# One elementwise product of 128x768 made in eight operations of 128x96, in the third layer of a graph network kernel

## What is computed

```python
def _L2_gnn_ref(feat, src, dst, W, b):
    m = jax.nn.relu(feat[src]) + EPS
    logits = BETA * m
    seg_max = jax.ops.segment_max(logits, dst, num_segments=N)
    ex = jnp.exp(logits - seg_max[dst])
    denom = jax.ops.segment_sum(ex, dst, num_segments=N)
    a = ex / denom[dst]
    msg = jax.ops.segment_sum(a * m, dst, num_segments=N)
    feats = feat + msg
    return feats @ W + b
x = _layernorm(x + _L2_gnn_ref(x, L2_gnn_W, L2_gnn_b, src, dst), axis=-1)
```

## Time and profile before

| | |
|---|---|
| median of 3 runs | 4265.86 us |
| lowest and highest | 4262.5 and 4268.29 us |
| span of the profiled execution | 4261.0 us |
| DVE busy, whole span | 2819.2 us (66%) |
| POOL busy, whole span | 2740.4 us (64%) |
| third layer, first gather to the end of the stage | 2443 to 3110 us |

### The profile page before, as it was taken

The page is one execution under the profiler, slowest core; times in us unless marked ns, Lnnn a source line. Parts: engine busy times, 40 slices in busy tenths (PEclk is TensorE's granted clock), DMA queues, the critical chain, the costliest instruction groups (busy, mean ns, idle before and its releaser), DMA issues. The chain is left out here.

```text
span 4261.0 us, 39832 instructions
## 1 busy us (share of the span) xinstructions
PE 1919.8 (45%) x8382; PEld 1417.5 (33%) x8382; DVE 2819.2 (66%) x10490; ACT 1859.7 (44%) x3815; POOL 2740.4 (64%) x2760
## 2 busy tenths in 40 slices
PE   5578634777766666644444357777710000000000
PEld 2244103666654554522222157777700000000000
DVE  8899854777765655568878767777655545454545
ACT  8699102656642222224444446565632323232323
POOL 7366656666646666656666466666457666676766
PEclk9899556877778777766666556666655555555555
DMA  1111764555545555545566444444322222222221
GB/s 51 49 35 36 213 203 111 145 135 138 143 122 178 181 173 177 179 139 181 180 187 185 145 135 164 152 157 158 125 77 72 65 72 68 68 69 67 72 65 51
DMA packets 380540, 524.65 MB, mean 123 GB/s; under 512 B 221914, under 2 KB 255983, under 8 KB 380042
## 3 DMA queue, kind: packets, MB, share of 16 engines
q1 hardware_dynamic: 286154, 366.89, 26.1%
q0 software_dynamic: 94144, 155.21, 15.4%
HBM read 230.36 MB, written 291.54 MB: 122 GB/s over the span
## 5 line engine op out<-in xcount | busy, mean ns | idle before, releaser
L1632 POOL DMA_INDIRECT l_G<-t,src x391 | 415.0, 1061 | 228.3 <-issue 104.6
L1949 POOL DMA_INDIRECT out<-O,nidx x392 | 393.4, 1004 | 229.3 <-issue 110.9
L1311 POOL DMA_INDIRECT l1a_G<-t,src x391 | 376.5, 963 | 232.1 <-issue 111.7
L2167 PE MATMUL l_psR<-l_diag,l_ones 128*128 128x128 f32 x2 | 0.8, 501 | 1131.2 <-DVE l_diag L2031 1131.2
L1932 POOL DMA_INDIRECT l_G<-t,src x391 | 403.2, 1031 | 166.7 <-issue 118.2
L1311 POOL DMA_INDIRECT l1b_G<-t,src x391 | 380.2, 972 | 197.7 <-issue 110.4
L642 POOL DMA_INDIRECT O<-x_pad,nidx x344 | 326.7, 950 | 188.9 <-DMA O<-x_pad,nidx 97.0
L975 POOL DMA_INDIRECT l_G<-xs,src x327 | 310.3, 949 | 169.0 <-issue 88.4
L2167 PEld LDWEIGHTS l_psR<-l_diag,l_ones 128*128 128x128 f32 x2 | 0.5, 310 | 1131.3 <-DVE l_diag L2031 1131.3
L207 ACT ACTIVATE O<-O,l_shift,l_rstd 128x96 f32<-128x96 f32 x784 | 291.2, 453 | 27.2 <-DVE l_shift L201 27.2
L1989 DVE TENSOR_TENSOR l_e<-l_G,l_to_score 128x8 f32<-128x8 f32 (+3 forms) x51 | 8.5, 166 | 444.2 <-DMA l_G<-t,src 444.2
(11 more groups left out here) (350 smaller groups left out, 6554.5 us busy)
## 6 DMA issues: line engine op xcount, KB each, us to landing
h<-l_G SPq DMA_DIRECT2D x96, 392.0 KB, 2.4
t<-l1b_t_out SPq DMA_DIRECT2D x48, 768.0 KB
h<-l_G SPq DMA_DIRECT2D x48, 768.0 KB, 3.8
xs<-en_y SPq DMA_DIRECT2D x48, 392.0 KB, 3.7
t<-l_t_out SPq DMA_DIRECT2D x48, 392.0 KB
l_H<-t SPq DMA_DIRECT2D x48, 392.0 KB, 3.2
en_y<-x_pad SPq DMA_DIRECT2D x48, 384.0 KB, 4.9
t<-l_tr_out SPq DMA_DIRECT2D x48, 384.0 KB
```

The costliest lines, as they stand in the source:

```text
L1311: pool.indirect_dma_start(tile(c)[:, q, :], None, table, bass.IndirectOffsetOnAxis(k.src[:, at:at + 1], 0))\
L1632: pool.indirect_dma_start(tile(c)[:, q, :], None, table, bass.IndirectOffsetOnAxis(k.src[:, at:at + 1], 0))\
L1949: pool.indirect_dma_start(out, bass.IndirectOffsetOnAxis(k.nidx[:, at:at + 1], 0), k.O[:, at, :], None, bounds_check=NP - 1, oob_is_err=Fa ...
```

## The change

```diff
@@ layer2, join(c) on DVE @@
                 u, n = c % 2, width(c)
                 v = inv[:, u, 0:n, :]
                 dve.wait_ge(inverted, c + 1)
-                dve.tensor_tensor(v, v, tile(c)[:, :, D:W2], ALU.mult)
+                for q in range(n):
+                    dve.tensor_tensor(inv[:, u, q, :], inv[:, u, q, :], tile(c)[:, q, D:W2], ALU.mult)
                 dve.drain()
```

## The result

The changed kernel takes 4277.0 us (median of 20 runs, 4263.81 to 4287.69), the kernel before 4267.24 us (20 runs, 4255.45 to 4272.72): a ratio of 1.0025, 95% interval 1.0015 to 1.0035. It is **slower by a quarter of a per cent**; forecast was 0.35% faster.

What follows compares the result with a forecast made beforehand. POOL's gathers and their landings were taken to bound the third layer. Gain 16.0 us, less 0.8 for eight other chunks and 0.3 at the end, is 14.9: 4265.9 - 14.9 = 4251 us, range 4244 to 4262 us.

Steps and rivals of the forecast that it cites:

- What bounds the layer: Third layer: POOL's loop of gathers and its own landings sets the pace, 414.0 + 104.6 + 95.3 = 613.9 us.
- The cost on DVE: Third layer: eight products take 1.40 us, 0.47 us longer per chunk, some 23 us busy, absorbed by 2.9 us slack.
- The sixth gather at 1.01 us: Third layer: the gather meeting the product falls from 1.576 to 1.01 us, saving 0.56 us in each of 40 chunks.
- Rival A: Third layer, starvation: eight products hold POOL to the group's end, 0.47 us more per gather, +19 us, 4285 us; chance 0.05.
- What is given back by the seventh and eighth gather: Third layer: both now fall into the masked additions L1680, costing 0.04 and 0.12 us per chunk.
- my 400: Third layer: busy time of the gathers (L1632) falls from 415.0 to about 400 us.
- The fourth layer starts when this one ends, so what is saved here is kept: Passage from third to fourth layer: the third layer's saving of 14.9 us carries through to the total.
- my forecast's mechanism: Third layer: shorter products let POOL's sixth gather in sooner, net 0.40 us per chunk over 40 chunks, 16.0 us.

Runs made afterwards that it cites:

- the four traces: Changed kernel; it with 44 memsets before layer four; that with products as scalar_tensor_tensor; changed kernel with both product inputs equal: 1.0025, 1.0008, 1.0013, last one run without ratio.

## Why the prediction was wrong, point by point

**What bounds the layer: right.** POOL's gathers, 0.3 us between them and 48 landings of 2.0 us make up the stretch before and after.

**The cost on DVE: right.** I took 1.40 us for eight products, and they took 1.40 us; 23 us more in all, and 69.6 less 46.6 is 23.0. The 0.47 us more per chunk lay in DVE's slack (waits for landings still 110.5 us).

**The sixth gather at 1.01 us: right in two thirds of the chunks, wrong in the third that counts.** This is the step that failed in the third layer. It is the bound: "0.94 us at one, 1.00 us at another, and 1.22 us at the worst of the 43 that meet these groups". I took 1.22 us for the worst that such a group can do. It was the worst only because a single operation was left in the group when the gather asked. The row didn't bound the wait, it bounded the rest of the group. With five left the wait is 1.06 us (2.01 less 0.95): 16 gathers at 2.01 us instead of 1.01 cost 16 us of the gain.

**Rival A had the right price and place, and 0.05 as its chance.** It said 0.47 us more than before per gather; 2.01 against 1.55 us is 0.46. It said all 40, and 16 to 26 were held, so that in the third layer it takes back most or all of the gain: 607.9, 615.5, 611.7 and 612.0 us in the four traces, against 614.9, 614.8 and 613.9 with one product. I had argued against it from a gather that met L1378 at another moment. That the whole kernel came out slower, as A said, is not A's doing: the third layer still gained 7.0 us, and the loss lies in the fourth.

**What is given back by the seventh and eighth gather: too high.** I put 0.16 us per chunk on it. In kernels where no gather is held the third layer's gathers are busy for 389.4 to 394.9 us, against my 400. With eight products and no gather held it gained 26.4 us in the trace (614.9 less 588.5), where I had 14.9.

**"The fourth layer starts when this one ends, so what is saved here is kept": this is the step that turned the sign.** It assumes that unchanged code keeps its pace. The fourth layer lost 16.6 us, since 340 more DVE records ahead of it moved a recurring delay of 0.3 us off the one instruction where it did good. The row was there (23 waits at L2009, 5.1 us in all), and I had looked at no line of the fourth layer. With the delay put back and the group moved by some 0.05 us, the same eight products give 0.9957, which is my forecast's mechanism and a little more than its size (0.43% in place of 0.35%).

What stays open: what DVE does at each 128th record (the profile says only that it waits for nothing it shows); why 27 of the 112 gathers at the critical moment got in; why at that moment a whole group can pass ahead of POOL; and why of 91 gathers that asked at the same distance after the start of the fifth L1378 none was held. Nor is it shown why the fourth layer's gathers take 3.6 us more in the changed kernel.

## What to carry to other kernels

Where POOL issues indirect DMAs beside DVE work with two inputs in SBUF, look at single gathers and not at their mean: each costs its own time, what is left of the DVE operation it meets, or what is left of the whole group. When a long operation is split to let POOL in, two or four pieces did it here, and in a single run a small operation without SBUF inputs between the pieces; eight in a row did it only when they met POOL's gather 0.05 us elsewhere. And a change that makes an engine's program longer can change code behind it: compare the untouched stages too, and before believing a small loss or gain, shift the program by a few idle instructions and see whether it stays.

## What was unexpected of the hardware

- Each 128th DVE record of the program starts some 0.3 us late where DVE isn't waiting anyway. In the fourth layer, whose chunk has 64 records, the place of this delay was worth 16 us or more: 1145.2 to 1163.5 us for the same instructions.
- Small DVE operations with two SBUF inputs, 0.17 us apart, held a gather of POOL from the third to the eighth (2.01 us against 0.95), though each lasts only 0.25 us. A gather that asked 0.14 to 0.16 us after a product's start wasn't delayed in 17 chunks, and the next product was put off in its place, to 0.08 us after the gather had asked.
- The result of a meeting hangs on some 0.05 us between the engines, and at the critical moment it isn't even fixed: 2.01 us in one chunk and 1.00 in another with the starts of group and gather 0.22 and 0.21 us apart.
- A delay on an engine with slack can shorten the program: two memsets ahead of the products, with the rest aligned, made the difference between 1.0008 [0.9997, 1.0020] and 0.9957 [0.9940, 0.9973].
